# Attention block: the update of x copied by ScalarE, the input rows added by accumulating GpSimd DMAs

## The reference, cut to what matters

```python
def _L0_conv_ref(x, ...):
    res_long = x
    xn = group_norm(x)                        # 8 groups
    t = conv1x1(xn, ciw) + cib + pe           # tokens [8, 4096, 64]
    tn = layer_norm(t)
    q2, k2, v2 = in_proj(q(tn), k(tn), v(tn)) # 8 heads of 8
    z = softmax(q2 k2^T / sqrt(8)) v2 @ wout.T + bout   # over the 8 images
    t = z + t
    a, g = layer_norm(t) @ w1.T + b1, t @ w2.T + b2
    t = a * gelu(g) @ w3.T + b3 + t
    y = t.transpose(0, 2, 1).reshape(b, c, h, w)
    return einsum('bchw,oc->bohw', y, cow) + cob[None, :, None, None] + res_long

def _L1_conv_ref(x, w1, b1, w2, b2):
    for _ in range(3):
        t = relu(conv3x3(x, w1) + b1)
        x = x + (conv3x3(t, w2) + b2) / 3
    return relu(x)
```

## Time and profile before

| | |
|---|---|
| three runs | 1140.28, 1140.54, 1140.69 us; median 1140.54 |
| span of the profiled execution | 1136.3 us |
| what lies around the span (median less span) | 4.2 us |
| setup block | 0 to about 44 us |
| attention block | about 44 to 604 us |
| convolutions | from about 604.7 us to the end |

### The profile page before, as it was taken

The page is one execution under the profiler, slowest core; times in us unless marked ns, Lnnn a source line. Parts: engine busy times, 40 slices in busy tenths (PEclk is TensorE's granted clock), DMA queues, the critical chain, the costliest instruction groups (busy, mean ns, idle before and its releaser), DMA issues. The chain is left out here.

```text
span 1136.3 us, 21019 instructions
## 1 busy us (share of the span) xinstructions
PE 1071.2 (94%) x7238; PEld 601.7 (53%) x7238; DVE 1039.7 (92%) x1475; ACT 652.5 (57%) x1525; POOL 510.7 (45%) x422
## 2 busy tenths in 40 slices
PE   4269999999999999999999999999999999999996
PEld 3156787778777777777653333333333333333331
DVE  5459999999999999999988999999999999999996
ACT  4568889888888888888743233253244242342333
POOL 5134564456445544554452424435345344444440
PEclk9999999999999999999999999999999999999998
DMA  8110111111111111110000000030001100030003
GB/s 303 54 37 21 39 29 35 32 39 29 33 35 38 29 31 38 38 29 20 20 20 1 1 1 1 1 75 1 1 1 34 41 1 1 1 74 1 1 1 74
DMA packets 87545, 35.83 MB, mean 32 GB/s; under 512 B 70210, under 2 KB 86851, under 8 KB 86931
## 3 DMA queue, kind: packets, MB, share of 16 engines
q1 hardware_dynamic: 85634, 33.81, 11.1%
q0 software_dynamic: 768, 0.33, 0.2%
q10 hardware_dynamic: 1040, 0.35, 0.1%
HBM read 26.09 MB, written 8.39 MB: 30 GB/s over the span
## 5 line engine op out<-in xcount | busy, mean ns | idle before, releaser
L1173 ACT ACTIVATE y<-banks,cols 128x1024 f32<-128x1024 f32 x96 | 110.3, 1208 | 259.8 <-PE banks L1165 259.8
L900 POOL TENSOR_TENSOR rstd<-var,half 128x8 f32<-128x8 f32 x32 | 80.8, 2526 | 216.5 <-DVE var L755 216.5
L1155 PE MATMUL banks<-mixed_h,cwp 128*128 128x512 f32 x384 | 177.6, 605 | 0.0
L1155 PE MATMUL banks<-early,cwp 128*128 128x512 f32 x372 | 169.2, 602 | 0.5 <-PEq L420 0.5
L1456 POOL TENSOR_TENSOR early<-xs 128x256 f32<-128x256 f32 x95 | 77.1, 811 | 160.1 <-DVE xs L1204 160.1
L1181 DVE TENSOR_TENSOR y<-y,banks 128x512 f32<-128x512 f32 x192 | 119.9, 682 | 15.2 <-ACT y L1173 15.0
L558 PE MATMUL banks<-consts,early 128*128 128x128 f32 x1024 | 133.2, 279 | 0.0
L1189 DVE TENSOR_TENSOR y<-y,banks 128x512 f32<-128x512 f32 x192 | 124.4, 685 | 8.7 <-PE banks L1165 6.5
L577 PE MATMUL banks<-consts,prod 128*128 128x128 f32 x1024 | 128.2, 273 | 2.8 <-DVE prod L526 2.1
L1155 PEld LDWEIGHTS banks<-mixed_h,cwp 128*128 128x128 f32 x384 | 69.0, 189 | 107.9 <-issue 107.9
L558 PEld LDWEIGHTS banks<-consts,early 128*128 128x128 f32 x1024 | 114.3, 144 | 18.8 <-issue 18.1
(11 more groups left out here) (184 smaller groups left out, 1868.8 us busy)
## 6 DMA issues: line engine op xcount, KB each, us to landing
xs<-in_x SPq DMA_DIRECT2D x4, 2048.0 KB, 16.5
xa<-in_x SPq DMA_DIRECT2D x32, 256.0 KB, 2.8
xr<-in_x SPq DMA_DIRECT2D x64, 128.0 KB, 2.8
out_y<-xs SPq DMA_DIRECT2D x32, 256.0 KB, 4.5
cw<-in_L_conv_w POOLq DMA_DIRECT2D x2, 144.0 KB, 3.9
consts<-in_consts ACTq DMA_DIRECT2D x1, 192.0 KB
group<-in_consts SPq DMA_DIRECT2D x1, 64.0 KB
w1n<-in_L_conv_w ACTq DMA_DIRECT2D x1, 64.0 KB
```

The source lines that it names most:

```text
L900: pool.tensor_tensor(rstd1[:, :], var1[:, :], top["half"][:, :], ALU.pow).then_inc(rstd1_done, 1)
L1155: pe.matmul(psum[PSUM_PAIR[v, q, j]][i][:, :, :], weights(v, i, j).rearrange("p n o -> p (n o)"), mixed[v][i][:, s0:s0 + WIDE, j, :], star ...
L1173: act.activation(pairs(y[i][q][:, :, :]), m1, ACT.Identity, bias=cols[:, (6, 8)[v]:(7, 9)[v]]).then_inc(m1_out[i][q], 1)
```

## The change

DVE's `dve_x` and SyncE's `sp_xr` go, with the two `xr` buffers. ScalarE copies the update with its bias from PSUM to `xs` (`act_x`, two activations of 128x256 a tile), one iteration later, between `act_gelu` and `act_z`. GpSimd waits for both, and issues two DMAs a tile that add the input rows from HBM onto `xs` (`accum_op=ALU.add`), between `pool_rstd2` and `pool_bias`. Each goes to 64 partitions, 8 images, 256 bytes a row: 512 rows of 256 bytes. `run` has one iteration more, and the block's end waits for the last of these DMAs. `written` waits for the DMAs in place of `x_done`.

```diff
-        def dve_x(dve, t, k, d):
...
-            wait(dve, cow_mm, t + 1)
-            dve.scalar_tensor_tensor(x_view(t, d), x_psum(d), cols[:, 4:5], xr_view(k, d), ALU.add, ALU.add).then_inc(x_done[d], 1)
+        def act_x(act, t, d):
+
+            wait(act, cow_mm, t + 1)
+            act.activation(x_view(t, d), x_psum(d), ACT.Identity, bias=cols[:, 4:5]).then_inc(x_done[d], 1)
+
+        def pool_residual(pool, t):
+
+            for d in range(2):
+                wait(pool, x_done[d], t + 1)
+            for r in range(2):
+                wait(pool, residual[r], 16 * t)
+                pool.dma_start(xs[half(r), :, t, 1:1 + HW], x_rows[:, :, 2 * t + r, :], accum_op=ALU.add)\
+                    .then_inc(residual[r], 16)
@@ written
-            for d in range(2):
-                wait(eng, x_done[d], 8 * (c + 1))
+            for r in range(2):
+                wait(eng, residual[r], 16 * 8 * (c + 1))
@@ act_iteration
             if tiles[4]:
                 act_gelu(act, t - 4, 0)
+            if tiles[5]:
+                act_x(act, t - 5, 1)
+                act_x(act, t - 5, 0)
             if tiles[3]:
                 act_z(act, t - 3)
@@ dve_iteration
-            if tiles[4]:
-                dve_x(dve, t - 4, (k - 4) % RING, 1)
...
-            if tiles[4]:
-                dve_x(dve, t - 4, (k - 4) % RING, 0)
@@ pool_iteration
             if tiles[4]:
                 pool_rstd2(pool, t - 4)
+            if tiles[5]:
+                pool_residual(pool, t - 5)
             if tiles[1]:
                 pool_bias(pool, t - 1, (k - 1) % RING)
@@ sp_iteration
-            if tiles[4]:
-                sp_xr(sp, t - 4, k - 4)
@@ run
-            for t in range(TILES + 5 - 1):
-                iteration(eng, t, t % RING, [0 <= t - s < TILES for s in range(5)])
+            for t in range(TILES + 6 - 1):
+                iteration(eng, t, t % RING, [0 <= t - s < TILES for s in range(6)])
@@ block.gpsimd
             run(pool, pool_iteration)
+            for r in range(2):
+                pool.wait_ge(residual[r], 16 * TILES)
```

More of the change, by code:

```diff
@@ L435, in attention_block @@
         tt = [sb(f"tt{k}", [P, N]) for k in range(RING)]
-        xr = [sb(f"xr{k}", [P, B, HW]) for k in range(2)]
         prod1 = top["early"][0][:, 0:HD * S].rearrange("p (e s) -> p e s", e=HD)
@@ L470, in half @@
             return slice(C * k, C * k + C)
-        xr_in = [sem("xr_in0"), sem("xr_in1")]
         edges_zeroed, pads_zeroed = sem("edges_zeroed"), sem("pads_zeroed")
@@ L486, in attention_block @@
         gated_done, x_done = [sem(f"gated_done{e}") for e in range(2)], [sem(f"x_done{e}") for e in range(2)]
+        residual = [sem(f"residual{r}") for r in range(2)]
         rstd1_done, rstd2_done, attn_done, rrep_done = sem("rstd1_done"), sem("rstd2_done"), sem("attn_done"), sem("rrep_done")
@@ L852, in x_psum @@
             return (b5, b7)[d][:, 0:PAIRS * HW].rearrange("p (q w) -> p q w", q=PAIRS)
-        def xr_view(k, d):
-            return xr[k % 2][:, 4 * d:4 * d + 4, :]
-        def dve_x(dve, t, k, d):
[L860 to L863, removed]
-            wait(dve, cow_mm, t + 1)
-            dve.scalar_tensor_tensor(x_view(t, d), x_psum(d), cols[:, 4:5], xr_view(k, d), ALU.add, ALU.add).then_inc(x_done[d], 1)
+        def act_x(act, t, d):
[8 more added lines that the diff above has]
+                    .then_inc(residual[r], 16)
         def x_piece(i, c):
@@ L915, in sp_xa @@
             sp.dma_start(xa[k % 2][:, :, :], x_pairs[:, :, bass.ds(t * TILE, TILE)]).then_inc(xa_in[k % 2], 16)
[L917 to L922, removed]
         def pe_iteration(pe, t, k, tiles):
```

## The result

The changed kernel takes 1303.55 us (median of 4 runs, 1302.86 to 1304.48) against 1140.41 us of the kernel before in the same runs: the ratio is 1.1434, interval 1.1418 to 1.145. It is slower by 163 us, where 108 were forecast; the forecast of 1248 us was 56 us too low, and the result lies just inside the range of 1214 to 1305 us.

What follows compares the result with a forecast made beforehand. TensorE and DVE bound the kernel about equally; the new loop of 17.96 us plus 2.0 for issues gives 19.96 us a period. 28 x 3.68 = 103 us, plus 4.3 at the joint, gives 1248 us, range 1214 to 1305.

Steps and rivals of the forecast that it cites:

- What bounds the kernel: Steady attention block: TensorE and DVE about equally late, period 16.28 us; taking work from DVE alone can give little.
- The wait ahead of the bias closes a loop: GpSimd waits for ScalarE's copy with the bias queued behind; period 17.96 us before issues; main case's chance 0.83.
- DVE's dense stretch: In the loop from `dve_z1` to `rstd2`: DVE's own order without idle, 8.78 us, not shortened by the lighter DVE.
- The wait of ScalarE before `act_z`: Sign expected in the profile after: ScalarE's idle of 0.99 us there shrinks to about 0.2 us.
- The issues, D: GpSimd's time for both DMA issues ahead of the bias: 2.0 us a tile taken, bounds 1.06 and 8.4.
- the 1221 us that the prediction worked out for this rule: Whole kernel's time if descriptor generation is small: both issues together 1.06 us, period 19.02 us.
- The clock: TensorE idling 4 us in 20 could lower its clock; granted clock 1.00 in the fill, so nothing was added.
- The joint: Attention block's end to convolutions: ScalarE's copies, GpSimd's issues and the last DMA's landing end it 4.3 us later.
- The count of 28: Iterations 5 to 32, where the DMAs stand ahead of a bias: 28 times 3.68 us gives 103 us.
- the issue did not grow eightfold with the rows: Rival on GpSimd's issues: price grows with rows, 8.4 us a tile, period 26.4, 1430 us; chance 0.10.
- the loop was longer than its sum and not shorter: Rival: DVE's stretch or ScalarE's tail closes up, each 0.5 us a period worth 14 us; near 1175; chance 0.02.
- DVE's relief decided nothing: Rival: bias not late, lighter DVE shortens the period about 0.3 us a tile, 1136 us; chance 0.03.

Runs made afterwards that it cites:

- The kernel without residual: The changed kernel without the DMAs and without GpSimd's wait, input rows added by nobody: 1137.88 us, ratio 0.999.
- the wait alone: The changed kernel without its DMAs, GpSimd still waiting for ScalarE's copy ahead of the bias: 1183.23 us, ratio 1.0389.
- the kernel with one DMA: The changed kernel with only the first of each tile's two DMAs, odd image rows getting no residual: 1258.23 us, ratio 1.1044.
- Five matmuls in the gap: The changed kernel with five matmuls on constants on TensorE ahead of its wait for `dve_z1`: 1272.32 us, ratio 1.1177.
- the kernel without the last pair: The changed kernel with wait and DMAs moved behind the bias, and the last tile's two DMAs left out: 1138.74 us, ratio 1.0.

## Why the prediction was right or wrong

**What bounds the kernel: right.** TensorE and DVE were taken as equally late, with little to win from DVE. The kernel without residual shows it: DVE 0.95 us lighter, the period still 16.28 us. DVE then waits 0.67 us for TensorE ahead of `dve_z1` and 0.31 us further up.

**The wait ahead of the bias closes a loop: right, and its length too.** 17.96 us was forecast without the issues, 17.88 measured with the wait alone. The bias at 2.40 us (2.36), DVE's dense stretch, ScalarE's copies at 0.80 us (0.88) all hold. The wait of ScalarE before `act_z` did not shrink to 0.2 us; it is 0.90 us.

**The issues, D: taken too small.** 2.0 us was taken. The two issues take 2.36 us, and the hand-over from ScalarE to an issue takes 0.3 us (copy ends 341.68, issue starts 341.98), not the 0.08 us of a computing instruction, which holds for ScalarE too (with the wait alone the copy ends at 317.29 and the bias starts at 317.37). In the loop they are worth 20.51 - 17.88 = 2.63 us in place of 2.0: 0.63 us a tile, 18 us in all, of which the slightly shorter loop (17.88 for 17.96) gives 2 back. That the adding form costs more held, 1.18 us against 0.70; that it is the reading of the destination which costs is the prediction's reason and no run separates it. The Trainium skill (DMA: Bandwidth & Descriptors, section "Anatomy of one DMA") calls the making of descriptors small. For plain DMAs that is near the truth here, 0.70 us for 512 rows against 0.53 for 64 small ones; for adding ones it is not, 1.18 us, and the 1221 us that the prediction worked out for this rule did not come.

**The clock: the step that failed.** The prediction ended that point with "so I put nothing there", on the ground that the granted clock was 1.00 in the fill. That was a misreading twice over. The value of 1.00 for the fill isn't borne out by the durations in the same trace, the one of the kernel before:

```profile
46.81 2.08 PE L547 MATMUL banks<-basis,tt 64*128 64x256 f32 x8 [1.34 <-ACT tt L688]
...
74.18 1.13 PE L547 MATMUL banks<-basis,tt 64*128 64x256 f32 x8 [0.45 <-ACT tt L688]
```

The same eight matmuls take 2.08 us four times up to 63.69 us, and 1.13 from 74.18 on, the same two durations as in the changed kernel at the lower and at the higher level. So the fill began at the lower level, and the price of it stood in the rows. And the row gives TensorE's share of busy time, 69%, where the change makes one pause of 3.43 us in every period. Behind it the granted clock is 0.54 for 3 us, `dve_var2` and `act_scores_t` wait for TensorE, and the loop grows by 1.43 us: 28 x 1.43 = 40 us, the larger part of the miss. The Trainium skill (TensorE: Matmul & The Clock Gate, section "Part 1: The HAM clock gate") states that an idle array runs at 1.2 GHz and a busy one at 2.4; the traces agree (0.50 and 1.00 in the kernel with one DMA), and with the price from the fill it should have made a case of its own.

**The joint: 4.3 us forecast, 4.9 measured,** and 2.0 us more in the convolutions, where nothing was forecast; the clock is lower there at first (0.87). **The count of 28 held nearly:** 156.2 us over 5.66 us a period is 27.6 periods. The period is 1.98 us longer than forecast, and of the miss of 56 us the steady part makes 53.

The range held the result only because it reached for a costlier issue, up to D = 4, and D is worth 2.63; that the number lies inside is luck, the width was there for another reason than the one that used it. **Of the rivals,** none came: the issue did not grow eightfold with the rows, the loop was longer than its sum and not shorter (by 0.08 us it was, with the wait alone), and DVE's relief decided nothing.

## What to carry to other kernels

Before a wait is put into an engine's list, follow the instruction that stands behind it: here a bias addition with 0.05 us of slack, and a loop through GpSimd, ScalarE, DVE and, once its clock falls, TensorE made 163 us of a change whose best case was 0.1%; one place further down the same wait and DMAs cost 7 us. When a forecast says that TensorE will stand still for some us in every period, price the clock at which it comes back as well, from rows on both levels, and check a clock value against the durations of like matmuls. An engine that is 97% busy is no bound in itself if another is just as late: the kernel without the work is the cheapest test of what its removal can bring.

## What the runs showed of the hardware

- Two costs that stay small alone can be large together: 44 us and 33 us alone, 163 us in a row. Each alone was paid for in part by the same 1.5 us of a faster bias and slack. TensorE's pause was 1.5 us and 0.8 us long alone, with the clock at 1.00 after it, and 3.4 us together, with the clock near one half.
- Periods can alternate between two lengths with identical instructions (19.31 and 21.65 us), by TensorE's clock: 1.00 behind a pause of 2.24 us, 0.50 behind one of 2.96. With plain DMAs a pause of 2.47 us was followed by a granted clock of 0.72 over 3 us, in a period of 20.48. Five matmuls in the gap left a pause of 1.8 us, with the clock at 1.00 behind it.
- The bias addition on GpSimd took 3.44 us with DVE at work beside it and 2.36 us with DVE idle.
- GpSimd's issue of a DMA of 512 rows of 256 bytes takes 0.70 us plain and 1.18 us accumulating. The next instruction's row starts before the issue ends: the bias behind it reads 3.26 us and took 2.36.
- ScalarE's copy to GpSimd's DMA issue takes 0.3 us to hand over, DVE or ScalarE to a computing instruction of GpSimd 0.08 us.
- The accumulating DMAs landed 3.9 us after their issue in the median, plain ones of the same rows 3.0 us from GpSimd and 2.8 us from SyncE. By the kernel without the last pair, the landing of the other 62 cost nothing.
